# A sorted gather and sum of graph rows: step-ordered rows, turns behind quarters of a tile, a deeper ring

## The reference, cut to what matters

```python
def _L0_gnn_ref(x, weight, row, col, vals):
    h = jnp.einsum('nf,ef->ne', x, weight)
    msgs = vals[:, None] * h[col]
    return jax.ops.segment_sum(msgs, row, num_segments=N_NODES)
...
x = x + _L0_gnn_ref(_layernorm(x, axis=-1), L0_gnn_weight, src, dst, edge_weight)
x = x + _L0_ffn_ref(_layernorm(x, axis=-1)[None], L0_ffn_W, L0_ffn_b)[0]
```

## Time and profile before

| | |
|---|---|
| median of 3 runs | 1632.9 us (1631.47 to 1633.22) |
| the profiled execution | 1631.87 us, its span 1630.0 us |
| PE, DVE, ACT, POOL busy | 93%, 69%, 34%, 66% |
| gathers (POOL L630) | 1024, 55.4% of the DMA engines' time |
| TensorE clock granted | 0.993 on average |

### The profile page before, as it was taken

How to read it: one execution, slowest core, us unless ns; L and a number is a source line. 1 busy time by engine, 2 the same in 40 slices (tenths; PEclk the granted TensorE clock), 3 DMA queues, 4 the chain that set the end, 5 groups by cost and what they waited for, 6 DMA issues and landing times.

```text
span 1630.0 us, 27821 instructions
## 1 busy us (share of the span) xinstructions
PE 1522.7 (93%) x3697; PEld 619.9 (38%) x3698; DVE 1116.9 (69%) x4106; ACT 556.9 (34%) x1223; POOL 1070.4 (66%) x1099
## 2 busy tenths in 40 slices
PE   7999998999989899999998999998999999999995
PEld 3444443444333234343333433333433333333442
DVE  8776648788877878888778777787433333336885
ACT  7887212222222222222222222222234444444332
POOL 2000257777777777777777777777777777777970
PEclk9999999999999999999999999999999999999998
DMA  9886687777999877789988777888877777777563
GB/s 334 300 280 227 213 271 216 205 202 220 307 309 302 285 202 207 199 251 324 309 297 257 207 215 202 246 258 253 252 206 212 209 210 210 208 210 203 181 208 110
DMA packets 162798, 387.79 MB, mean 238 GB/s; under 512 B 32642, under 2 KB 51362, under 8 KB 162466
## 3 DMA queue, kind: packets, MB, share of 16 engines
q0 software_dynamic: 81920, 268.50, 55.4%
q1 hardware_dynamic: 57666, 75.51, 13.8%
q10 hardware_dynamic: 23040, 41.95, 7.7%
HBM read 335.54 MB, written 55.57 MB: 240 GB/s over the span
## 4 chain that ended last, share of the span: by engine, by line
PE 80%; DVE 10%; issue 5%; DMA 2%; DVEq 2%; ACT 0%; POOL 0%; SPq 0%; POOLq 0%; ACTq 0%
PE psum L1452 60%; PE psum L1318 14%; PE psum L1484 3%; DVE rows L1064 3%; DMA rows<-h_rows,rows 2%; DVE rows L964 2%; DVEq L1064 1%; DVE rows L950 1%; DVE rows L956 1%; DVE rows L1144 1%; PE psum L1328 1%; PE psum L1334 1%; DVE rows L962 1%; DVE rows L958 1%; DVE rows L1209 0%
## 5 line engine op out<-in xcount | busy, mean ns | idle before, releaser
L630 POOL DMA_INDIRECT rows<-h_rows,rows x1024 | 1007.7, 984 | 506.2 <-issue 399.3
L1452 PE MATMUL psum<-rows 128*128 x2552 | 1186.2, 608 | 77.5 <-DVE rows L1064 35.3
L1452 PEld LDWEIGHTS psum<-rows 128*128 128x128 f32 x2552 | 443.8, 189 | 775.3 <-issue 767.4
L1064 DVE SCALAR_TENSOR_TENSOR rows<-rows 128x128 f32 (+1 forms) x1276 | 444.9, 351 | 384.4 <-PE psum L1452 271.8
L792 ACT ACTIVATE rows<-psum 128x512 f32<-128x512 f32 x128 | 76.4, 597 | 479.3 <-PE psum L1452 479.3
L1318 PE MATMUL psum<-rows 128*128 128x512 f32 x512 | 223.2, 593 | 0.8 <-ACT rows L689 0.8
L964 DVE COPY_PREDICATED rows<-rows 128x256 f32<-128x256 int32 x407 | 179.7, 442 | 0.0
L774 ACT ACTIVATE psum<-rows 128x512 f32<-128x512 f32 x256 | 153.7, 601 | 8.0
L950 DVE TENSOR_TENSOR rows<-rows 128x128 int32<-128x128 f32 x452 | 129.5, 287 | 19.8 <-ACT rows L708 18.2
L1318 PEld LDWEIGHTS psum<-rows 128*128 128x128 f32 x512 | 96.0, 190 | 114.7 <-issue 114.7
L962 DVE TENSOR_TENSOR rows<-rows 128x128 f32<-128x128 f32 x452 | 128.8, 285 | 0.2
(11 more groups left out here) (152 smaller groups left out, 493.1 us busy)
## 6 DMA issues: line engine op xcount, KB each, us to landing
rows<-in_x_blocks SPq DMA_DIRECT2D x32, 512.0 KB, 4.4
rows<-in_x SPq DMA_DIRECT2D x16, 1024.0 KB, 7.2
h_rows<-rows SPq DMA_DIRECT2D x64, 256.0 KB, 2.9
rows<-h_rows,rows POOLq DMA_INDIRECT x1024, 3.9
summed_rows<-rows ACTq DMA_DIRECT2D x64, 256.0 KB, 5.4
rows<-summed_rows ACTq DMA_DIRECT2D x64, 256.0 KB, 4.4
out<-rows SPq DMA_DIRECT2D x4, 2816.0 KB, 10.7
rows<-in_x ACTq DMA_DIRECT2D x32, 256.0 KB, 5.3
```

Source lines behind the costliest of these rows:

```text
L630: pool.indirect_dma_start(into[:, (c + 1) % n_slots, :], None, h_dram, bass.IndirectOffsetOnAxis(ap=dst_i[g][:, i:i + 1], axis=0),).then_i ...
L1064: dve.scalar_tensor_tensor(spread[:, slot % SR, :], iota_n[:, bass.ds((tile - (g * T + 1)) * P, P)], src_f[g][:, bass.ds(chunk - (g * NC + ...
L1452: pe.matmul(banks[:, bass.ds(pe.snap(tile_wanted) % AGG, 1), :].rearrange("p t f -> p (t f)"), spread[:, slot % SR, :], landed_in[:, bass. ...
```

## The change

- `WIDE` is 46 and `RING` 14. `wT` moves out of the ring's place, and `xT` lies under its last 8 slots, so chunks 0 to 36 may be gathered in stage 1 and chunk 37 waits for its last tile. The place for it comes from the table `iota_n`, 1023 numbers wide where it was 8192. A gather in stage 1 waits for the deviations of that x tile alone whose place it takes.
- The farthest row that part 0 wants is found by POOL (a cast, a `tensor_reduce` over all axes, a cast) where VectorE and TensorE found it. At least 36 tiles of h are waited for. `FILLED` is 36: the late rows of `h_rows` are filled with 14 copies of two tiles where there were 10, two at a time.
- Turns stand behind quarters of an h tile (one block) where they stood behind whole tiles. ACT copies nothing back: VectorE copies the upper half of the turned keys and reads the rest in PSUM.
- Flips from the eighth on are done ahead of the turn, by signs that differ by partition.
- Rows and weights come in the order of the steps: a new sum (`steps summed`, five matmuls 320 wide) makes `step_rows` and `step_weights`. A build reads a fixed column and a fixed table `row_q`, with no registers. `source` is gone.
- `plan` has new numbers, `HEAD` goes further, and `LAST_STEPS` is 64.

```diff
-    RING = 10
+    RING = 14
-    FILLED = 44
+    FILLED = 36
-    LAST_STEPS = 40
+    LAST_STEPS = 64
...
-        turn, tile, start = 0.9, 3.43, 15.5
+        turn, of_block, back, start = 0.75, 0.8575, 0.8, 15.5
...
-                    while n < T - 1 and tensor + tile / 2 < vector:
-                        tensor, n = tensor + tile, n + 1
+                    while n < KD * T - 2 and tensor + of_block / 2 < vector:
+                        tensor, n = tensor + of_block, n + 1
...
+            pool.wait_ge(s_edge[0][1], 16)
+            pool.tensor_copy(far_f, dst_i[0]).then_inc(s_far_f, 1)
+            pool.wait_ge(s_far_f, 1)
+            pool.tensor_reduce(far_one[:, :], far_f, mybir.AxisListType.XYZWC, ALU.max).then_inc(s_far, 1)
...
                 if c == 0:
-                    pool.wait_ge(s_sd, LOADS)
                     near_rows_stored()
-                if c + 1 == T - KEPT:
+                if KEPT + c + 1 < T:
+                    pool.wait_ge(s_sd, (KEPT + c + 1) // LT + 1)
+                if c + 1 == WIDE - XS:
                     pool.wait_ge(s_mm, T)
...
-                        if turns <= BY_SCALAR[g]:
-                            dve.wait_ge(s_key_in[g], turns)
-                        else:
-                            weights_now = turned_weights
-                            dve.wait_ge(s_turn_k[g], turns)
-                            dve.tensor_copy(keys_now, turned_keys).then_inc(s_key_in[g], 1)
-                            dve.wait_ge(s_key_in[g], turns)
+                        weights_now, is_turned = turned_weights, True
+                        dve.wait_ge(s_turn_k[g], turns)
+                        first = 6 if j else k - 1
+                        dve.tensor_copy(pairs(keys_now, first)[1], pairs(turned_keys, first)[1]).then_inc(s_key_in[g], 1)
+                        dve.wait_ge(s_key_in[g], turns)
...
+            def sum_steps(g):
+                pe.wait_ge(s_fin[g], 3)
+                rows_sum, share_sum = bank(ROW_BANK)[:, 0:NSP], bank(SHARE_BANK)[:, 0:NSP]
+                pe.matmul(rows_sum, turned_src[:, 0:P], step_hots[:, 0, :], start=True, stop=False)
+                pe.matmul(rows_sum, turned_src[:, P:NC], step_hots[:, 1, :], start=False, stop=False)
+                pe.matmul(rows_sum, ones[0:T, :], over, start=False, stop=True)
+                pe.matmul(share_sum, turned_wgt[:, 0:P], step_hots[:, 0, :], start=True, stop=False)
+                pe.matmul(share_sum, turned_wgt[:, P:NC], step_hots[:, 1, :], start=False, stop=True).then_inc(s_stair[g], 1)
```

More of the change, by code:

```diff
@@ L96, in sort_slots @@
         yield "index", 0, 0
-        yield "source", 0, 0
-        for what in ("maxima", "counts", "rows"):
+        for what in ("maxima", "counts", "rows", "steps"):
             yield what + " summed", 0, 0
@@ L105, in gnn_ffn, with flips_behind @@
     SORT_SLOTS = list(sort_slots())
-    ON_TENSOR = ("turn", "maxima summed", "counts summed", "rows summed")
+    ON_TENSOR = ("turn", "maxima summed", "counts summed", "rows summed", "steps summed")
     assert sum(what == "turn" for what, _, _ in SORT_SLOTS) == TURNS
     assert sum(what == "weights" for what, _, _ in SORT_SLOTS) % 2 == 1
+    def flips_behind(k, j):
+        return k >= 7 and k < QB and j == 0
     def plan():
-        vector_times = {"pack": 6.0, "flip": 0.3, "keys": 0.65, "weights": 0.65, "turned": 1.9, "maxima": 2.5,
-                        "counts": 2.0, "rows": 2.0, "index": 0.4, "source": 0.8}
-        turn, tile, start = 0.9, 3.43, 15.5
+        vector_times = {"pack": 6.7, "flip": 0.38, "keys": 0.6, "weights": 0.556, "turned": 0.0, "maxima": 3.6,
+                        "counts": 2.0, "rows": 3.2, "steps": 1.0, "index": 0.4}
+        turn, of_block, back, start = 0.75, 0.8575, 0.8, 15.5
+        tile = KD * of_block
         vector, tensor, n, behind, inverts, b = 3.0, start, 0, [], [], 0
-        end = start + T * tile + turn * (TURNS + 3)
+        end = start + T * tile + turn * (TURNS + 4)
         head, is_open = 0, False
         for g in range(2):
-            for at, (what, _, _) in enumerate(SORT_SLOTS):
+            for at, (what, k, j) in enumerate(SORT_SLOTS):
                 if g and vector > end - 12.0 and not is_open:
@@ L134, in plan @@
                 vector += vector_times.get(what, 0.0)
+                if what == "weights" and flips_behind(k, j):
+                    vector += 0.25
                 inverts.append(0)
-                while b < LOADS and (vector > start + (b * LT + 1) * tile or what in ON_TENSOR and b <= n // LT):
+                while b < LOADS and (vector > start + (b * LT + 1.7) * tile or what in ON_TENSOR and b <= n // (KD * LT)):
                     inverts[-1], b = inverts[-1] + 1, b + 1
@@ L150, in gnn_ffn @@
     assert FIRST_HOTS + QT // 2 < FIRST_PACK
-    BEHIND_TILE, INVERTS, HEAD = plan()
-    HEAD_TURNS = sum(what == "turn" for what, _, _ in SORT_SLOTS[:HEAD])
+    BEHIND_BLOCK, INVERTS, HEAD = plan()
     def slots_with_steps():
@@ L1382, in of_sort @@
                     sum_rows(g)
+                elif what == "steps summed":
+                    sum_steps(g)
             turn_w()
@@ L1386, in _ @@
                 multiply(n)
-                for tile, g, what in BEHIND_TILE:
-                    if tile == n:
-                        of_sort(g, what)
             def turn_layer(l):
```

206 lines of the change are left out of this document (110 added, 96 removed).

## The result

| | kernel before | kernel after |
|---|---|---|
| median of the timed runs, us | 1632.18 (1630.73 to 1633.22, 4 runs) | 1709.39 (1692.82 to 1714.64, 4 runs) |
| ratio, 95% interval | | 1.0456 [1.0383, 1.053] |
| profiled execution, its span, us | 1631.87, 1630.0 | 1707.0, 1705.3 |

Slower by 4.6%, 75 us, where I forecast 1634.0 and a range up to 1641. The prediction was wrong, and not by a rival that it names. In what follows the kernel after's lines are its own: gathers L662 (before L630), steps L1481 (L1452), blocks of stage 1 L1338 (L1318), turns L1350 and L1354, builds of a step's matrix L1085 (L1064), a compare stage of the sort L978, L982, L984, L988, L994.

The account below looks back on a forecast made before the run. POOL's gathers were taken to bound the kernel, released by stage 1's end. Ring -7.7, end of stage 1 +10.5, start +0.6 and POOL's pace -2.3 made +1.1 us, forecast 1634.0 us, range 1627 to 1641.

Parts of the forecast that it names:

- What bounds the kernel: Stage 2: from 790 us on POOL's gathers, 1.287 us each, set the pace; VectorE and TensorE have slack.
- The ring, -7.7: Gathers in stage 1: 37 chunks out instead of 31, six more at 1.287 us, -7.7 us; POOL then waits some 35 us.
- The end of stage 1, +10.5: TensorE's last tile, which releases POOL: four more turns +1.8, fourth sum +3.2, waits at turns +5.5, ending at about 255.8 us.
- The start, +0.6: Set-up: POOL's new reduction over all axes, taken as 2 us, holds VectorE and delays the start by 0.6 us.
- the estimate of 31: Start: a Trainium skill figure scaled by columns gives 31 us for POOL's reduction; the total would be near 1663 us.
- the rival that rested on it: Start: POOL's reduction holds VectorE, 1639 us at 6.95 us of reduction; chance 0.19, and 0.04 for over 10 us.
- POOL's own pace, -2.3: Gathers beside sorting cost about 0.033 us more; 34 of 349 compare stages move ahead of stage 2, -2.3 us (0 to -4).
- The tail, fixed: After the last gather: the time to the end was taken as a fixed tail, unchanged.
- In stage 2, "gain 0, loss 0": Cheaper builds and narrower turn copies on VectorE, and 3 us more TensorE work a part, stay behind POOL's clock: 0.
- The sum without that step: Whole kernel: the terms -7.7, +10.5, +0.6 and -2.3 summed to +1.1 us.
- All my rivals for "slower": POOL's reduction holding VectorE, 1639 us (0.19) or beyond (0.04); gathers' run-ahead in stage 1 not growing, 1642 us (0.03).
- the signs that I named for being wrong: Stage 1 ending before 251 or after 261 us, POOL waiting for steps, or TensorE's lead never falling to some 5 chunks.

Follow-up runs that it names:

- e9: Kernel after with register work and dynamic addresses ahead of builds, POOL's normalising paced, and each turn one block later: 1638.74 us, ratio 1.0005.
- e2: Kernel before with its builds reading fixed columns, without registers (output not the reference's): 1712.6 us, ratio 1.0441.
- e1: Kernel after with register work and dynamic addresses put back ahead of each build: 1643.83 us, ratio 1.0047.
- e7: Kernel after with POOL waiting for its own previous instruction before each normalising one in the tail: 1691.91 us, ratio 1.0362.
- e6: e1 with four more register operations ahead of each build, seven in place of three: 1645.4 us, ratio 1.0071.
- e3: Kernel after with the weights' copy in each compare stage written as a maximum of the weights with themselves: 1760.45 us, ratio 1.0721.
- e4: Kernel after with RING 10 in place of 14: 1715.49 us, ratio 1.0488.
- e10: Kernel after with register work ahead of each build but a dynamic address in one build of eight only: 1708.92 us, ratio 1.0422.
- e11: Kernel after with fixed builds and a dynamic address on the weights' copy instead; no register operation in its trace: 1714.44 us, ratio 1.047.
- e5: Kernel after with e1's three register operations but fixed columns in builds; its trace has none of the operations: 1701.12 us, ratio 1.0429.

## Why the prediction was wrong

- **What bounds the kernel**: right. POOL's gathers set the pace before and after, and 231 of them from 1170 to 1460 us stand in both.
- **The ring, -7.7**: right. 37 gathers were out, the wait was 35.1 us, no other long one came.
- **The end of stage 1, +10.5**: right, chunk 37 at 256.33, and so are the parts. A turn without a wait moves the next block by 0.437 us; the 19 turns moved it by 14.07 us in all, which is 1.7 for the four new ones and 5.8 of waits, where the sum had 1.8 and 5.5. The fourth sum cost 3.1 us and the others 0.7 more than before, against 3.2. In all stage 1 ends 11.0 us later (255.58 and 244.59). TensorE's weight loads waited some 17 us at turns, not 4 to 7, but most of that lies beside running blocks. The 5.8 us come from the planner, which puts turns too early: in e9 they are 0.1.
- **The start, +0.6**: the reduction took 0.80 us, not 2, nor the estimate of 31, and the first block of stage 1 started at 15.07 us, before at 15.32; the rival that rested on it falls.

```profile
7.53 0.80 POOL L610 CROSS_LANE_REDUCE far_one<-rows 128x1 f32<-128x256 f32 x1
...
9.17 0.88 DVE L1074 TENSOR_SCALAR rows<-rows,w_sum 128x512 f32<-128x512 f32 x2 [0.89 <-ACT w_sum L690]
```

- **POOL's own pace, -2.3: the step that failed**, in its last sentence: "I count the register-free builds at nothing for POOL, since their matrix instruction stays." The matrix instruction stays, but the pause ahead of it goes. I had the price of VectorE's sort on POOL (1.289 against 1.255 us) and took it for a price by compare stage that stays what it is. It hangs on how VectorE's row is spaced: 986 gathers from chunk 37 on took 1.343 us each, not 1.29, which is +55 us. e2 shows that this edit alone does it, e1 that undoing it takes back 66 us with the tail.
- **The tail, fixed**: wrong in this execution, +17.3 us. I had not asked what else may run beside POOL's row of 64 instructions. e7 shows the cause. What decides whether an execution meets it stays open. The kernel before has the same two rows side by side, and in its profile, as in those of e1 and e6, no hot tile took over 0.82 us; of the unpaced kernels without pauses in the builds the profiles of after, e2, e3, e4, e10 and e11 have one of 16 us or more (e2, e3, e10 and e11 a second of 12.5, with tails of 127 us), that of e5 none. The sort is over by then, and nothing that I ran ties the one to the other.
- **In stage 2, "gain 0, loss 0"**: TensorE waits 61.0 us for builds, 35.3 before, but POOL still sets the pace, as the 272 chunks beside 271 gathers show, so that costs nothing, as forecast.
- **The sum without that step.** With the pause back the kernel is 1.0047 of before, +7.7 us, where the sum had +1.1, or +3.4 without the term that failed. By the starts of gathers it is +3.3 at chunk 37, +4.4 at 256 and +9.2 at 740: the mechanism of the other terms was right, and some 5 us are a pace of 1.303 in place of 1.294 us. Why e1 is that much slower stays open: the longer pauses of e6 did not mend it.

The range failed because no rival put a price on VectorE having less to do. All my rivals for "slower" were things that the change adds. And of the signs that I named for being wrong none appeared; only the expected 1.28 to 1.29 us a gather and the last start at 1522 to 1524 did not hold.

## What to carry to other kernels

Where a GpSimd that starts DMAs sets the pace, VectorE's pauses are part of the schedule: before removing register work, waits or idle slots from VectorE, look at how its row is then spaced, price that by a gather beside such a row, and compare the period of VectorE's loop with a held-up gather and what follows it: 1.66 us against 1.67 was the bad case here. Builds without register work cost 5 to 6% of the pace, one pause of 0.1 us in each 1.85 us takes it back, and more than that buys nothing. A run that adds register work says something only if the trace has that work: in two of mine it had not. A long row of GpSimd can hold VectorE for many instructions, so pace it with a wait for itself where the other is on the path.

## What was not expected of the hardware

- A gather on GpSimd took 6.41 us (median 0.946) beside five compare stages of VectorE without a pause, and a VectorE instruction of 0.27 us took 18.904 us beside 25 GpSimd instructions of 757 ns back to back. The first wait ended with VectorE's first pause (0.80 us from there to the gather's end), the second while GpSimd's row went on. Beside builds a gather gets in without any pause.
- Register operations cost VectorE's stream nothing that shows until an instruction takes an address from them: 0.20 us from L984 to the build with two register operations and fixed columns (e10, 197 of 214), 0.37 with dynamic ones (e1).
- A row of gathers and a row of compare stages fall in step, 1.66 against 1.67 us, and each gather is then held up at the same place.
- A reduction of GpSimd over all axes of 128x256 took 0.80 us.
